# A graph kernel's build stage: own products spread over two tiles, splits moved off GpSimd, and the first degree tree in a buffer of its own

## The reference

```python
# layer 0, twice (W0, b0, then W1, b1); rows = src, cols = dst
deg = segment_count(rows); vals = 1 / max(deg, 1)[rows]
neigh = segment_sum(vals[:, None] * x[cols], rows)
x = relu(concat([x, neigh]) @ W.T + b)
# then x = layernorm(x_in + x)
# layer 1
h_self, h_neigh = feat @ W_self, feat @ W_neigh
h_sparse = keep the 32 largest of each row of h_neigh, zero the rest
neigh = segment_sum(h_sparse[src], dst) / max(in_degree, 1)[:, None]
x = layernorm(feat + h_self + neigh)
```

## Time and profile before

| | us |
|---|---|
| median of 3 runs (750.69 to 753.83) | 751.52 |
| the profiled execution | 751.57 |
| its span from first to last instruction | 749.8 |
| TensorE busy | 643.7 (86%) |
| VectorE busy | 542.5 (72%) |
| GpSimd busy | 370.2 (49%) |
| ScalarE busy | 333.0 (44%) |

### The profile page before, as it was taken

One profiled execution on the slowest core, in us unless ns is written; L12 is line 12 of the kernel. 1 busy time (PEld: TensorE's weight loads), 2 busy tenths in 40 slices (PEclk: granted clock), 3 DMA queues, 4 the chain that ended last, 5 costly groups with the idle time before them and its releaser, 6 DMA issues.

```text
span 749.8 us, 11481 instructions
## 1 busy us (share of the span) xinstructions
PE 643.7 (86%) x4048; PEld 348.3 (46%) x4049; DVE 542.5 (72%) x1235; ACT 333.0 (44%) x597; POOL 370.2 (49%) x379
## 2 busy tenths in 40 slices
PE   2635388777778499999999999999999989999996
PEld 2624376666654144444444444444444434444443
DVE  7686499999982788888888446887787762744343
ACT  2122398888873377667676423333333320100000
POOL 2008999999985888888888122223223210000000
PEclk9955799999998599999999999999999989999999
DMA  9301346545553011010111155555555523320000
GB/s 229 48 3 45 92 146 203 149 146 147 160 159 84 14 35 38 32 42 29 42 30 40 28 148 178 169 157 176 176 165 160 172 55 106 111 80 21 28 22 27
DMA packets 39831, 72.99 MB, mean 97 GB/s; under 512 B 3609, under 2 KB 32496, under 8 KB 39770
## 3 DMA queue, kind: packets, MB, share of 16 engines
q1 hardware_dynamic: 39770, 72.20, 33.2%
HBM read 38.81 MB, written 33.38 MB: 96 GB/s over the span
## 4 chain that ended last, share of the span: by engine, by line
PE 54%; DVE 29%; POOL 5%; DMA 5%; issue 3%; ACT 2%; SPq 1%; DVEq 0%; POOLq 0%; ACTq 0%
PE pair L1453 27%; DVE hots L791 12%; PE bank L1541 9%; PE pair L1541 9%; DVE ct L797 5%; PE bank L1362 5%; PE pair L1362 3%; DMA xs<-in_x_dram 3%; DVE tree L868 2%; DVE tree L867 1%; PE bank L1368 1%; POOL w_scaled L480 1%; POOL w_parts L484 1%; POOL w_parts L481 1%; DMA own_in<-own_dram 1%
## 5 line engine op out<-in xcount | busy, mean ns | idle before, releaser
L1453 PE MATMUL pair<-xs,ct 125*128 125x512 f16 x625 | 146.5, 386 | 0.0
L1453 PE MATMUL pair<-a,ct 125*128 125x512 f16 x625 | 142.8, 379 | 0.0
L1059 ACT ACTIVATE slab<-pair 125x875 f16<-125x875 f32 (+1 forms) x100 | 105.3, 1090 | 48.3 <-PE pair L1331 42.9
L791 DVE TENSOR_TENSOR hots<-iota,jobs 128x1792 f16<-128x1792 f16 (+1 forms) x100 | 112.1, 1124 | 1.5 <-issue 1.5
L1453 PEld LDWEIGHTS pair<-xs,ct 125*128 125x128 f16 x625 | 61.7, 101 | 69.7 <-issue 3.6
L1453 PEld LDWEIGHTS pair<-a,ct 125*128 125x128 f16 x625 | 61.0, 99 | 68.1
L1158 ACT ACTIVATE a<-ct 125x1000 f16<-125x1000 f16 (+1 forms) x75 | 80.2, 1069 | 9.5 <-POOL tr_sb L549 8.6
L563 POOL TENSOR_TENSOR part<-t,part 125x256 f16<-125x256 f32 x25 | 16.7, 670 | 118.7 <-ACT part L1198 118.7
L1354 PE MATMUL bank<-ident,slab 125*128 125x125 f16 x625 | 53.2, 225 | 25.1 <-DVE ct L797 23.2
L1541 PE MATMUL bank<-xs,ct 125*128 125x512 f16 (+1 forms) x325 | 71.5, 379 | 0.0
L797 DVE COPY ct<-bank 125x882 f16<-125x882 f16 (+1 forms) x100 | 55.4, 556 | 20.2 <-PE bank L1354 20.2
(11 more groups left out here) (196 smaller groups left out, 1087.8 us busy)
## 6 DMA issues: line engine op xcount, KB each, us to landing
c_dram<-slab SPq DMA_DIRECT2D x25, 683.6 KB
ct<-c_dram SPq DMA_DIRECT2D x25, 683.6 KB
own_in<-own_dram SPq DMA_DIRECT2D x50, 125.0 KB
own_dram<-own SPq DMA_DIRECT2D x25, 125.0 KB
own_dram<-own_st SPq DMA_DIRECT2D x25, 125.0 KB
x_in<-in_x_dram SPq DMA_DIRECT2D x25, 125.0 KB
z_dram<-z_st SPq DMA_DIRECT2D x25, 125.0 KB
a<-z_dram SPq DMA_DIRECT2D x5, 625.0 KB
```

What stands on the lines that cost most here:

```text
L791: v.tensor_tensor(hots[k][:, :, :, :].rearrange("p w g (a d) -> p (w g) a d", d=2), iota, job, ALU.is_equal).then_inc(win_hot, 1)
L1059: a.activation(slab3[t % 2][:, :, lo * QW:hi * QW].rearrange("p b (w d) -> p w b d", d=QW), pair[f % 2][0:P, 0:n, 0:QKEY].rearrange("p w ( ...
L1453: ins = mm(agg[k % 3][0:lhs.shape[1], :], lhs, parts[l][:, t, :], start=t == 0, stop=t == NT - 1, skip_group_check=True)
```

## The change

- The x split is gone from GpSimd. x tile t is transposed in fp32 straight from `xs32` (two transposes with a new identity `identx`, into `xp`), ScalarE writes the high part with the scale (`own_t`), VectorE the low part from the same PSUM (`own_low`). The weights are split in the same manner by `w_high` on ScalarE (two after each of tiles 1 to 3) and `w_low` on VectorE (two in each of tiles 2 to 4). GpSimd keeps `split_a0` only.
- The own product of a tile is spread over two: turn and split in one tile, the product in the next. A table `OWN` says which are multiplied in which tile.
- ct copies: groups `TG` of 5, 8, 5 and 7 blocks in place of 7, 6, 6 and 6. ScalarE takes the first and third, VectorE the second and fourth. `tr_free` becomes one semaphore per bank.
- `quick_copy` goes over blocks, then windows, in place of windows, then blocks.
- Scale arithmetic: fewer and wider steps; the clearing of two PSUM banks comes earlier, and a set of one-hots stands between `bounds` and `scales_out`.
- TensorE and ScalarE have the general path first, so their jump over it comes ahead of the build. VectorE keeps the quick one first.
- The tree of block 0 is summed by VectorE into `tree0`, which lies in the not yet used `a1`; GpSimd starts with block 1. The long sums no longer wait for degrees(0). SP loads the first own tiles and the bias ahead of the last slab's store; the waits for all stores move to the first instruction that overwrites what they read.

```diff
-XC = [0, 9, 17, 25]
+XC = [0, 13, 25]
+OWN = {0: [], 1: [], 2: [], 3: [0], 4: [1], 5: [2], 6: [3, 4], 7: [5], 8: [6, 7], 9: [8], 10: [9, 10],
+       **{t: [t] for t in range(11, NT)}}
-TG = [7, 6, 6, 6]
+TG = [5, 8, 5, 7]
...
+            sp.wait_ge(tr_done, 4 * (NT - 1) + 1)
             load_own(0, 0)
             load_bias(0, b0)
             load_own(0, 1)
+            store_slab(NT - 1)
+            sp.wait_ge(w_stored, 32)
+            sp.wait_ge(own_done, NT)
             load_w(0)
...
             pool.sem_inc(a0_split, 2)
-            split_x(0)
-            split_w(w_t[0], w0_parts, 3, w0_split, 1)
...
+            for t in range(NT):
+                split_a0(t)
...
-            pool.wait_ge(tr_free, 4 * NT + 2)
-            sum_tree(0)
+            for done in tr_free:
+                pool.wait_ge(done, 2 * NT + 1)
...
+            def w_low(i):
+                dve.wait_ge(w_hi, i + 1)
+                hi, lo, w, by = halves(i)
+                v.scalar_tensor_tensor(lo, w, by, hi, ALU.mult, ALU.subtract).then_inc(w_split, 1)
+            def own_low(t):
+                dve.wait_ge(own_tcopied, t + 1)
+                v.scalar_tensor_tensor(x_t16[:, 2:4, 0:P], xp, scales[:, 0:1], x_t16[:, 0:2, 0:P], ALU.mult, ALU.subtract
+                                       ).then_inc(own_tlo, 1)
...
                 for t in range(1, NT):
-                    for g in range(4):
-                        tr_copy(t - 1, g)
-                        if t + 1 < NT:
-                            quick_hots(t + 1, g)
+                    more, own = t + 1 < NT, OWN[t]
+                    if more:
+                        quick_hots(t + 1, 0)
+                    tr_copy(t - 1, 1)
...
+            dve.wait_ge(own_done, NT)
+            first = [region[0][:, 5 * PC * k:5 * PC * (k + 1)] for k in range(5)]
+            step(v.tensor_tensor(tree0, first[0], first[1], ALU.add))
+            for k in range(2, 5):
+                step(v.tensor_tensor(tree0, tree0, first[k], ALU.add))
             end_tree(0)
...
-                a.activation(slab3[t % 2][:, :, lo * QW:hi * QW].rearrange("p b (w d) -> p w b d", d=QW),
-                             pair[f % 2][0:P, 0:n, 0:QKEY].rearrange("p w (b d) -> p w b d", d=QW),
+                a.activation(slab3[t % 2][:, :, lo * QW:hi * QW].rearrange("p b (w d) -> p b w d", d=QW),
+                             pair[f % 2][0:P, 0:n, 0:QKEY].rearrange("p w (b d) -> p b w d", d=QW),
...
             def own_t(t):
                 act.wait_ge(own_tp, t + 1)
-                a.activation(x_t16[:, :, 0:P], tp[2], ACT.Copy).then_inc(own_tcopied, 1)
+                a.activation(x_t16[:, 0:2, 0:P], xp, ACT.Copy, scale=scales[:, 0:1]).then_inc(own_tcopied, 1)
...
+            def own_transposes(t, rows_):
+                for h in range(2):
+                    last = nc.tensor.transpose(xp[:, h, :], rows_[:, h * 128:(h + 1) * 128], identx[:, :])
+                last.then_inc(own_tp, 1)
...
-            pe.wait_ge(tr_free, 4 * NT + 2)
-            degrees(0)
+            for free in tr_free:
+                pe.wait_ge(free, 2 * NT + 1)
             pe.wait_ge(a0_split, NT + 2)
             for T in range(2):
                 aggregate(0, T, NT - 2, NT)
+            degrees(0)
+            aggregate(0, 2, 0, 9)
             degrees(1)
-            aggregate(0, 2, 0, 9)
             turn_h(0)
-            degrees(2)
             aggregate(0, 2, 9, 17)
             product(0)
+            degrees(2)
```

More of the change, by code:

```diff
@@ L137, in gnn @@
         x_t16 = bld("x_t16", [128, 4, 128], F16)
[L138 to L139 removed]
+        identx = bld("identx", [P, P], F32)
+        xstage = bld("xstage", [P, F], F32)
         own = bld("own", [P, 2, 2 * F], F32)
+        slab = [bld(f"slab{i}", [P, SLAB], F16) for i in range(2)]
+        slab3 = [t[:, 0:N].rearrange("p (b d) -> p b d", d=P) for t in slab]
         held = [Arena(ct_at + (b * REG + HELD * PC) * 2, ct_at + (b + 1) * REG * 2) for b in range(19, NT)]
@@ L318, in store_own @@
                 sp.dma_start(own_dram[t], own[:, t % 2, 0:F]).then_inc(own_stored[t % 2], 16)
-            for t in range(NT):
+            for t in range(NT - 1):
+                for o in OWN[t]:
+                    store_own(o)
                 store_slab(t)
[L322 to L325, removed]
+                if t == HELD - 2:
+                    sp.wait_ge(w_split, 6)
                     for l in range(2):
@@ L1091, in quick_copies @@
                         act.wait_ge(w_stored, 32)
-                    for f in range(FILLS):
-                        quick_copy(t, f)
-                        if f == 1:
-                            own_t(t - 1)
-                    own_copy(t - 1, (t - 1) % 2, (t - 1) // 2)
+                    own = OWN[t]
+                    quick_copy(t, 0)
+                    tr_copy(t - 1, 0)
+                    quick_copy(t, 1)
+                    if own:
+                        own_copy(own[0], own[0] % 2, own[0] // 2)
+                    if t == 2:
+                        own_t(0)
+                    if own and own[0] + 1 < NT:
+                        own_t(own[0] + 1)
+                    quick_copy(t, 2)
+                    tr_copy(t - 1, 2)
+                    quick_copy(t, 3)
+                    if len(own) > 1:
+                        own_copy(own[1], own[1] % 2, own[1] // 2)
+                        own_t(own[1] + 1)
+                    if t == 1:
+                        ready_for_own()
+                    if t < 4:
+                        w_high(2 * t - 2)
+                        w_high(2 * t - 1)
+                for g in (0, 2):
+                    tr_copy(NT - 1, g)
             def copies():
@@ L1101, in copies @@
                 ready_for_own()
+                for i in range(6):
+                    w_high(i)
                 for m0, m1 in ((0, HELD // 2), (HELD // 2, NT // 2)):
```

267 lines of the change are left out of this document (139 added, 128 removed).

## The result

The changed kernel takes 728.5 us (median of 4 runs, 724.33 to 729.79; a fifth that is on record took 727.7), the kernel before 751.33 (4 runs, 750.69 to 753.83). The ratio is 0.968, with a 95% interval of 0.9642 to 0.9718. The forecast was 710.5 with a range of 702 to 727: the sign was right, the gain is 23 us and not 41, and the median lies outside the range.

What follows compares the result with a forecast made beforehand. VectorE was taken to set the 5.96 us build tile, with GpSimd's splits delaying the start. Terms -20.5, -8.4, -1.1 and -11.0 sum to -41.0 from 751.57: 710.5 us forecast, range 702 to 727.

Steps and rivals of the forecast that it cites:

- start, to F0(4): Up to the first fill of tile 4: without GpSimd's splits, both TensorE waits (6.29 and 11.16 us) go, -20.5 us.
- F0(4) to F0(24): From tile 4's first fill to tile 24's: 20 tiles in 110.8 us against 119.15, -8.4.
- last tile: Last tile, with no one-hots behind it: ScalarE ends it after 5.0 us instead of 6.1, -1.1.
- E to the sums for block 3: After E, the end of tile 24's last slab copy: earlier bias, block 0's tree on VectorE, no 1.80 gap, -11.0 us.
- thus VectorE is the bound at 5.35: Steady tile: VectorE 5.17 us plus 0.18 held up by GpSimd; TensorE 4.5 and ScalarE 4.8 lie below.
- rival B: Slab copies cost what they did, ScalarE sets the tile at 5.75 us; total 721.5, chance 0.30.
- The rule on short reads: Slab copies: PSUM's 8-byte lines need two hits for full rate, so reads in pieces of 5 pay; supports rival B.
- Double tiles: Tiles 6, 8 and 10, with two own products each: TensorE 4.5 + 1.5, ScalarE waiting for the second, 6.3 us a tile.
- VectorE still jumps at the end: Behind the build: VectorE's branch over the general path stays there, while TensorE's and ScalarE's move to the start; no price given.
- C: Rival: GpSimd's cast and subtraction each stop a VectorE one-hot set, tile 6.24 us; total 727, chance 0.12.
- D: Rival: ScalarE's slab-copy reads in jumps of 5 cost more than the writes did; slower, 773 us, chance 0.04.
- E: Rival: no change to speak of, the GpSimd waits at the start only hid others; chance 0.02.

Runs made afterwards that it cites:

- Both edits that made the tile shorter: Changed kernel, VectorE's own low part behind the third one-hot set (727.58 us; from tile 11 only, 724.76); or ScalarE's x turn ahead of its product copy (722.02).
- ScalarE's swap: Changed kernel with ScalarE's x turn ahead of its copy of the product: 722.02 us, ratio 0.9621; added to four other edits together: 718.74 us.
- the two edits of the kernel before: Kernel before with only the new element order in slab copies: 750.63 us; with only x(2) to x(4) split ahead of the layer weights on GpSimd: 747.86.
- reordering: Kernel before with GpSimd's splits of x(2) to x(4) ahead of the weights for the layers: 747.86 us, ratio 0.9971.

## Why the prediction was wrong

By its own terms, all from profiled executions (751.57 before, 724.33 after):

| term | forecast | measured |
|---|---|---|
| start, to F0(4) | -20.5 | -22.5 |
| F0(4) to F0(24) | -8.4 | +3.3 |
| last tile | -1.1 | +0.3 |
| E to the sums for block 3 | -11.0 | -6.6 |
| layers | 0 | -1.9 |
| sum (by spans) | -41.0 | -27.3 |

The median is another 4.2 above the profiled execution.

- **Start: right**, for the reason given. Of its surplus 1.7 us are owed back, since the weights' low parts fell into tiles 3 to 5 and not 2 to 4, and tiles 4 and 5 were that much longer than forecast.
- **Steady tile: the step that failed is "thus VectorE is the bound at 5.35".** I compared the engines' sums and took the largest. VectorE's steps were right when nothing holds them (5.11 measured for 5.17). But GpSimd's hold was put at 0.18, inside bounds of 0 and 0.48, and is 0.42 in this kernel, though GpSimd has two operations instead of five. And moving the own low part to VectorE closed a ring through three engines that sums can't show; it makes VectorE wait, which costs 0.14. Together the tile is 5.67. 12 tiles x 0.31 = 3.7 of the 11.7 us missed. Both edits that made the tile shorter took off some of each, so the two shares are read from the trace and not from a run of their own. The copy's price was right in kind: 0.835 for 750 elements, not 1.06, so rival B is false, though the line through the earlier trace rows had given 0.79 and ScalarE is busy 5.12 a tile for 4.8. The rule on short reads that stands beside B did not come out: the copy that reads in pieces is the faster one. That passage of the Trainium skill (SBUF — State Buffer, on "cachelines") stands under Door 1 and not Door 3, gives the two hits for SBUF alone, and speaks of matmuls where it comes to PSUM, so it did not bear on this copy as the prediction had it.
- **Double tiles: mis-sized.** 6.3 was TensorE's sum with a wait; they took 7.68, 8.70 and 7.54, 5.0 us too much in all, of which 1.15 is the wait for the weight store in tile 8. With ScalarE's swap and a later wait for that store they take 6.8 to 6.9, so 0.7 a tile hung on the order of these steps, and some 0.5 stays unexplained. Tiles 4 and 5 (6.66 and 6.65 for 6.3 and 5.35) add 1.7, and the single tiles 7, 9 and 11 (5.76 for 5.35, cause open) add 1.2; with the steady ones that makes 11.6.
- **Last tile: -1.1 failed**: the chain there shows that ScalarE's own copy, released by the product behind that ring, stands ahead of its last copies.
- **Behind the build: two steps failed.** The bias landed as forecast (E + 6.3 for 7.8) and block 1 was summed at E + 13.5 (14.0). "VectorE still jumps at the end" was named and given no price, because the row that shows a jump was TensorE's 1.80; VectorE's took 6.62. And block 0 on VectorE was priced at 0.82 an addition with GpSimd at work beside it. The Trainium skill (SBUF — State Buffer, on the shared port pair) says that the engine which comes first blocks the other. The prediction weighed that rule only for the one-hots; the traces agree with it here, 1.88 for an addition that takes 0.82 alone, and 0.29 for a step of 126 elements alone but up to 1.42 beside GpSimd. With the jump out of the way and block 1 ahead of the bias one trace reached the forecast of E + 34.2 (34.4); another with the same code took 36.1.
- **How firm the -6.6 is.** It rests on one trace of each kernel. The sums for block 3 came at E + 38.6 to 40.7 in five traces with the changed kernel's code behind the build, and at E + 43.0 to 45.2 in three with that of the kernel before. So the gain there is 2.3 to 6.6, and the pair compared above gives the most. In the changed kernel's family the stretch from degrees(1) to these sums shows two lengths (the run with the store held back aside): 16.8 to 17.3, with a mean granted clock of 0.80 to 0.88 from E + 22 on, and 18.06 with 0.68 to 0.70. From the sums for block 3 to the end it is 479.6 to 482.8 us in all fifteen traces, 480.6 and 480.7 in the two edits of the kernel before, so the -1.9 for the layers can't be told from chance.
- **Rivals.** C holds in part: GpSimd stretches one set a tile to 1.37, and not two as C had it. It has 0.42 of C's 1.07, so that the measured time lies near C's 727 is luck. C's own sum is also off by a little: 6.24 less 5.35 is 0.89 and not 0.85, which gives 728. D and E are false.
- **The 4.2 us between the profile and the median.** Two profiles with the sums for block 3 at the same time (242.53 in the changed kernel, 242.47 with block 0 on GpSimd) end at 722.5 and 724.9. They differ first in the granted clock around it. The changed kernel from 240 to 245 us:

```profile
240.00:245.00 5.00, 3.89 (x20) 1.90 (x21) 4.22 (x12) 2.37 (x5) 4.24 (x4) 1.00 0.12 32
```

and the one with block 0 on GpSimd:

```profile
240.00:245.00 5.00, 5.00 (x13) 1.72 (x14) 4.34 (x8) 2.37 (x5) 4.23 (x4) 0.50 0.14 44
```

20 matmuls against 13, at the upper level (2.4 GHz) and at the lower (1.2). TensorE had waited 3.12 us just before in both. Of the 2.4 us, 1.5 are there when the next product for the degrees starts, at 248.25 and at 249.77. The other runs of the changed kernel have a mean clock of 0.957 to 0.965 and the profiled one 0.970. That all 4.2 us are clock is likely, not shown: of those runs there is no trace.

## What to carry to other kernels

Sum each engine's work for a tile, but then walk once around the loop by dependence, from a buffer that comes free back to the instruction that frees it, through the queue order of every engine; the tile is the longer of the two. When work moves to the busiest engine, ask what stands behind it in that queue and what it waits for. Ask too which steps of two engines that hold each other up will now fall together: a swap on a third engine can move them apart. A wait that an overloaded engine causes is worth its whole backlog, not its own length: reordering gave 0.6 us by tile 10, taking the work away gave 15.7. And before a term of a few us is read from one trace of each kernel, compare traces that have the same code in that stretch.

## What the runs showed of the hardware

- The same jump over a long unused path cost TensorE 1.80 us, and VectorE 2.9 at the start, 4.92 behind the build with a DMA share of 0.18 and 6.6 to 7.9 with one of 0.53 to 0.74.
- A ScalarE copy of 750 fp32 from PSUM to fp16 in SBUF takes 1.057 us when it writes in pieces of 5 elements and 0.835 when it reads PSUM in pieces of 5 and writes 30 in a row (0.817 in the kernel before). The short piece costs on the writing side; by the line through plain copies (0.79) the reading side pays at most 0.05.
- Beside GpSimd a VectorE operation loses 0.4 to 1.2 us whatever its length, so short ones suffer most in proportion: a set of 1536 elements is stretched from 0.94 to 1.37 by a GpSimd step, an addition of 630 from 0.82 to 1.8, a step of 126 elements from 0.29 to 1.2 to 1.5.
